# Two elementwise additions of GpSimd, moved from two and three to five and six slots behind their loads

## The chip, the cores and the metric

One core of one Trainium2 chip runs the whole program in one launch. The metric is the time of the execution on the device in microseconds (us), the median over several runs. The kernel before takes 2609.1 us (three runs, 2608.78 to 2609.54).

## What is computed

The reference is a small language-model tower over 64 x 256 = 16384 tokens of width 128, cut here to what matters:

```python
h = take(tok_weight, x)                                # embedding
h = h + linear_attention(layernorm(h))                 # layer 0
h = h + expert_choice_ffn(layernorm(h))                # 32 experts, top 512 tokens each
h = h + causal_attention(layernorm(h))                 # layer 1: 8 heads of width 128, t = 256
# layer 1 feed-forward: each token goes to the 2 best of 8 experts
logits = x @ gate_w + gate_b
w, idx = top_k(logits, 2); w = softmax(w)
out = sum over the two of w * (relu(x @ w1[e] + b1[e]) @ w2[e] + b2[e])
return h + out
```

The last step is the one that the change touches: for each token the two weighted expert rows are added, and the attention's result h is added to that as residual.

## The kernel before

The program is one fixed order per engine, written out by hand, with semaphores between the engines. It has three stages: layer 0 (up to about 900 us), then causal attention and, beside it, layer 1's experts, and a tail in which the last experts run alone.

The second stage is counted in **slots** `u`. Slot u belongs to sequence n = u // 8 and head h = u % 8; two sequences make a group g of 512 tokens (`TG = 4` tiles of 128), so a group is 16 slots. `U = 512` slots hold all heads of all 64 sequences. Every engine has a loop over u and does its part of the slot. For one head: TensorE multiplies the scores (lines 2052, 2053), VectorE takes the maxima (lines 1550, 1551), ScalarE the exponentials (lines 1081, 1083) and refills the mask (line 1091), the rows are scaled by VectorE (lines 1561, 1564; in slots up to 257 GpSimd does this, lines 900 and 901), TensorE transposes them (line 2064), VectorE copies the transposed rows out of the bank (line 1571), and TensorE multiplies them with the values (lines 2076 to 2078). The transposes of one head wait until the copy of the head before is done, so a late line 1571 holds TensorE at line 2064. VectorE also does the norm before attention (small steps in slots with h = 1, 2, 3), and the gate of a finished group (slots with h = 5, 6, 7 of its first and h = 3 to 7 of its second sequence; lines 1213 to 1223 are the steps of an inverse square root, lines 1627 to 1634 the mask, 1640 to 1649 the weights).

The routed rows of a group are scattered by GpSimd to regions of the 8 experts (`scatter`, line 865). The groups are cut into five **portions** (`PORTS`: groups 0 to 13, 14 to 21, 22 to 26, 27 to 29, 30 to 31). When a portion's groups are routed, its **units** (128 rows of one expert) run, one per slot: `place_steps` gives slots 256 to 377 to portion 0, 384 to 457 to portion 1, 464 to 513 to portion 2, and the rest to the tail. For a unit SyncE loads rows and weights four slots ahead (`load_unit`, lines 657 and 659), TensorE multiplies (lines 2092, 2096, 2104), ScalarE and VectorE finish (lines 1117, 1733), and GpSimd scatters the 128 results to `zbuf` two slots behind (`give_unit`, line 880).

When a portion is done, the **results** of its groups are formed. `RESULT_AT` maps a slot to the group c whose data is then loaded: slots 384, 388, ... 436 for groups 0 to 13, and 464, 468, ... 492 for groups 14 to 21 (one every four slots), later ones from slot 526 on. At that slot SyncE runs `turn_result(c)`: it waits until result c-2 is complete, stores it, and issues the loads of group c's expert rows (`zx`, 512 KB, line 687) and of the residual (`h3x`, 256 KB, line 688). GpSimd adds in two steps, each of four instructions of 128 x 128 float32: `add_rows` two slots behind (line 889, waits for the loads), `add_residual` three slots behind (line 895). Both buffers are double (c % 2). Results whose slot is 512 or later are added by VectorE, `LATE = 10` slots behind (lines 1743, 1745).

GpSimd's queue in a slot is, in this order: `residual` at h = 0 (line 874, two instructions that add the output bias for the sequence), `normalise` (early slots only), `scatter` (h = 1 to 4), `give_unit`, `add_rows`, `add_residual`. `give_unit` waits for VectorE's line 1733 of the slot before, so GpSimd follows VectorE slot by slot.

Of the kernel before, what the change touches and what calls it, by code (L numbers as in the profile page):

```python
# [86 lines left out]
def lm_tower(nc, x, L0_tok_weight, L0_attn_Wqkv, L0_attn_temperature, L0_attn_Wproj, L0_attn_bproj,  # L87
# [3 lines left out]
    with ExitStack() as ctx:  # L91
# [391 lines left out]
        def gated(i):  # L483
            return 0 <= i < NG

        STEPS, STEP_AT, STEP_END = place_steps()
        U = NB * H1
# [33 lines left out]
        RESULT_AT = {}  # L521
        for k, (g0, g1) in enumerate(PORTS[:-1]):
            for g in range(g0, g1):
                RESULT_AT[STEP_END[k] + ((6 + 4 * (g - g0)) if k < NKA - 1 else (12 + 6 * (g - g0)))] = g
        LATE = 10
        assert list(RESULT_AT.values()) == list(range(PORTS[-1][0]))

        def rounds(eng, one):
# [196 lines left out]
        def _(pool):  # L725
# [134 lines left out]
            def scatter(g, k, j):  # L860
                if k == 0 and j == 0:
                    pool.wait_ge(twice, 16 * (g + 1))
                    pool.wait_ge(pos_ready, g + 1)
                pool.nop(nofuse=True)
                pool.indirect_dma_start(out=spread_rows, out_offset=bass.IndirectOffsetOnAxis(ap=pos[:, k, j:j + 1], axis=0),  # L865
                                        in_=xr4s[g % 2][:, k, j], in_offset=None).then_inc(spread, 16)

            def residual(n):
                i, p = n // 2, n % 2
                pool.wait_ge(h2_in[p], 16 * (i + 1))  # L870
                if n >= 2:
                    pool.wait_ge(h3_ready, n - 1)
                for j in range(2):
                    ins = pool.tensor_tensor(hb[:, p, j], hx[:, p, j], bo[:], ALU.add)
                ins.then_inc(hb_ready, 1)

            def give_unit(t):
                pool.wait_ge(yu_ready, t + 1)
                pool.nop(nofuse=True)
                pool.indirect_dma_start(out=zbuf, out_offset=bass.IndirectOffsetOnAxis(  # L880
                    ap=xu_at(t)[:, C + 1:XW].bitcast(U32), axis=0), in_=yu[:, t % YR], in_offset=None,
                    bounds_check=2 * NTOK - 1, oob_is_err=False).then_inc(z_out[t % YR], 16)

            def add_rows(c):
                pool.wait_ge(z_in[c % 2], 32 * (c // 2 + 1))
                if c >= 2:
                    pool.wait_ge(out_done[c % 2], 16 * (c // 2))
                for j in range(TG):
                    ins = pool.tensor_tensor(res[:, c % 2, j], zx[:, c % 2, j, 0:C], zx[:, c % 2, j, C:2 * C], ALU.add)
                ins.then_inc(res_step, 1)  # L890

            def add_residual(c):
                pool.wait_ge(res_step, c + 1)
                for j in range(TG):
                    ins = pool.tensor_tensor(res[:, c % 2, j], res[:, c % 2, j], h3x[:, c % 2, j], ALU.add)
                ins.then_inc(res_ready, 1)

            def normalise(u, h):
                pool.wait_ge(rinv_ready, u + 1)
                pool.tensor_scalar(pr[:, u % PRN, 0:P], pr[:, u % PRN, 0:P], rinv[:, h % 4, 0:1], None, ALU.mult)  # L900
                pool.tensor_scalar(pr[:, u % PRN, P:3 * P], pr[:, u % PRN, P:3 * P], rinv[:, h % 4, 1:2], None, ALU.mult)\  # L901
                    .then_inc(pr_ready_pool, 1)

            for u in range(NI * 2 * H1):
                n, h = u // H1, u % H1
                i, p = n // 2, n % 2
                if h == 0 and n < NB:
                    residual(n)
                if 0 <= u - N_LAG < POOL_NORM:
                    normalise(u - N_LAG, (h - N_LAG) % H1)  # L910
                if gated(i - 2) and i <= NG and 1 <= h <= TG:
                    if u - 1 <= U:
                        pool.wait_ge(exp_ready, u - 1)
                    scatter(i - 2, p, h - 1)
                if i == NG + 1 and p == 0:
                    scatter(NG - 1, h // TG, h % TG)
                if u - 2 in STEP_AT and STEPS[STEP_AT[u - 2]][2] is not None:
                    give_unit(STEPS[STEP_AT[u - 2]][2])
                if u - 2 in RESULT_AT and u < U:
                    add_rows(RESULT_AT[u - 2])  # L920
                if u - 3 in RESULT_AT and u <= U:
                    add_residual(RESULT_AT[u - 3])
            for q in range(YR):
                pool.wait_ge(z_out[q], given(UNIT0[NK], q))

# [241 lines left out]
        def _(dve):  # L1167
# [507 lines left out]
            def split(n, p):  # L1675

                dve.wait_ge(xT3_ready, n + 1)
                dve.tensor_tensor(x_part[1][:, p], xT3[:, p], x_part[0][:, p].bitcast(F32), ALU.subtract).then_inc(parts_split, 1)  # L1678
# [58 lines left out]
            def results(c):  # L1737
                p = c % 2
                dve.wait_ge(res_ready, c)
                dve.wait_ge(z_in[p], 32 * (c // 2 + 1))  # L1740
                if c >= 2:
                    dve.wait_ge(out_done[p], 16 * (c // 2))
                dve.tensor_tensor(res[:, p], zx[:, p, :, 0:C], zx[:, p, :, C:2 * C], ALU.add).then_inc(res_step, 1)
                dve.wait_ge(res_step, c + 1)
                dve.tensor_tensor(res[:, p], res[:, p], h3x[:, p], ALU.add).then_inc(res_ready, 1)

            def slots(i):
                for p in range(2):
                    n = 2 * i + p
                    for h in range(H1):  # L1750
# [45 lines left out]
                        for k in range(NK):  # L1796
                            if i == PORTS[k][1] + 1 and p == 0 and h < TABLE_PARTS:
                                table(k, h)
                        if u - LATE in RESULT_AT and u - LATE >= U:
                            results(RESULT_AT[u - LATE])  # L1800
            split(0, 0)
# [413 lines left out]
```

## Time and profile before

| | |
|---|---|
| median of three runs | 2609.1 us (2608.78 to 2609.54) |
| the profiled execution, its own time | 2601.45 us |
| its span, first to last instruction | 2599.7 us |
| TensorE / VectorE / ScalarE / GpSimd busy | 2262.5 / 1832.7 / 1685.6 / 1546.0 us |
| mean granted TensorE clock | 0.941 of full speed |
| line 889, GpSimd | 88 instructions (22 results x 4), 1996.8 to 2389.5 us |
| line 895, GpSimd | 88 instructions, 1999.7 to 2392.4 us |

How to read it: the profile is of one execution. Busy times are sums of instruction durations; an engine that is idle but not awaited costs nothing. The stretch in which GpSimd adds results is 1990 to 2400 us, the tail runs from about 2410 us to the end. TensorE's clock has two levels, 1.2 and 2.4 GHz; a granted clock of 1.00 is the higher one.

### The profile page before, as it was taken

Reading aid. Unit: us, or ns where it says so; the run is one execution under the profiler, and the core shown is the slowest. Engines: PE = TensorE matmul, PEld = TensorE weight load, DVE = VectorE, ACT = ScalarE, POOL = GpSimd, SP = SyncE. Lnnn points to the kernel's source line nnn. Section 1 sums busy time; section 2 is a strip of 40 time slices with the busy share of each in tenths; the row PEclk is TensorE's granted clock in tenths of the full one; section 3 lists DMA queues with packets and bytes.
Section 4 is the critical chain, followed back from the end, with each engine's and each line's share of the span. In section 5 each row is a group of like instructions: output and inputs, shape, how many; then the busy total and the mean of one; then the engine's idle time right before and its main releaser. Section 6 shows DMA issues by size and latency. Waiting matters only on the chain.

```text
span 2599.7 us, 59052 instructions
## 1 busy us (share of the span) xinstructions
PE 2262.5 (87%) x16671; PEld 2024.2 (78%) x16687; DVE 1832.7 (70%) x8212; ACT 1685.6 (65%) x5272; POOL 1546.0 (59%) x1870
## 2 busy tenths in 40 slices
PE   4999877676666599999999999999999999999954
PEld 3887765455555498988989899999999888999854
DVE  4887756644444378888888887877778888888622
ACT  3777654222222377777777778888888777888743
POOL 6444100688888568888888874444444666456553
PEclk9999989777777799999999999999999999999987
DMA  2333200344444521110111126555554776477687
GB/s 81 101 91 98 85 22 1 65 73 74 74 74 74 112 60 35 33 35 30 34 36 31 35 80 164 158 161 153 157 158 139 208 215 199 110 224 218 173 258 241
DMA packets 304259, 283.98 MB, mean 109 GB/s; under 512 B 33931, under 2 KB 252651, under 8 KB 303936
## 3 DMA queue, kind: packets, MB, share of 16 engines
q1 hardware_dynamic: 254144, 211.15, 29.7%
q0 software_dynamic: 46336, 61.16, 10.2%
q10 hardware_dynamic: 3456, 7.89, 1.0%
q8 instruction: 138, 2.26, 0.4%
q14 instruction: 185, 1.52, 0.2%
HBM read 185.85 MB, written 88.43 MB: 106 GB/s over the span
## 4 chain that ended last, share of the span: by engine, by line
PE 53%; POOL 17%; DVE 14%; issue 9%; DMA 4%; SPq 2%; ACT 1%; DVEq 0%; POOLq 0%; ACTq 0%
POOL hbuf L831 8%; PE bank L2053 7%; PE bank L2143 6%; PE bank L2129 6%; PE bank L2064 5%; PE bank L2052 4%; PE bank L2096 4%; PE bank L2104 4%; PE bank L2078 4%; PE bank L2077 4%; PE bank L2076 4%; POOL xe L823 3%; POOL vo_place L791 2%; POOL pc L791 2%; PE bank L1936 1%
## 5 line engine op out<-in xcount | busy, mean ns | idle before, releaser
L880 POOL DMA_INDIRECT zbuf<-pc,kb x248 | 248.7, 1003 | 261.4 <-DVE pc L1733 213.1
L865 POOL DMA_INDIRECT spread_rows<-kb,pos x256 | 254.7, 995 | 167.7 <-DVE pc L1733 82.6
L1081 ACT ACTIVATE pr_place<-bank,nmax 128x128 f32<-128x128 f32 x512 | 188.0, 367 | 186.7 <-DVE nmax L1551 186.2
L2053 PE MATMUL bank<-xT,gT 128*128 128x256 f32 x1024 | 306.8, 381 | 0.0
L1571 DVE COPY pr_place<-bank 128x384 f32<-128x384 f32 x512 | 281.4, 550 | 11.2 <-PE bank L2064 10.6
L2064 PE MATMUL bank<-ident,pr_place 128*128 128x128 f32 x1536 | 252.7, 273 | 29.9 <-DVE pr_place L1571 29.8
L2064 PEld LDWEIGHTS bank<-ident,pr_place 128*128 128x128 f32 x1536 | 195.8, 141 | 100.8 <-POOL pr_place L901 20.0
L1550 DVE TENSOR_REDUCE nmax<-bank 128x1 f32<-128x128 f32 x512 | 143.9, 281 | 181.6 <-PE bank L2053 176.8
L2143 PE MATMUL bank<-wvo_part,x_part 128*128 128x512 f32 x768 | 269.6, 459 | 0.0
L1091 ACT ACTIVATE bank<-causal 128x384 f32<-128x384 f32 x512 | 253.4, 495 | 19.7 <-PE bank L2187 3.6
L2129 PE MATMUL bank<-x_part,wqk_part 128*128 128x256 f32 x1536 | 245.6, 296 | 1.2 <-DVE x_part L1678 1.2
L1083 ACT ACTIVATE pr_place<-bank,nmax 128x256 f32<-128x256 f32 x512 | 242.1, 473 | 0.0
L901 POOL TENSOR_SCALAR pr_place<-pr_place,rinv 128x256 f32<-128x256 f32 x256 | 235.7, 921 | 0.0
L831 POOL DMA_INDIRECT hbuf<-ye,idx x128 | 204.0, 1594 | 45.6 <-issue 38.1
L900 POOL TENSOR_SCALAR pr_place<-pr_place,rinv 128x128 f32<-128x128 f32 x256 | 155.3, 607 | 123.4 <-DVE rinv L1557 118.2
L823 POOL DMA_INDIRECT xe<-xrow,idx x128 | 125.2, 978 | 165.8 <-DVE idx L1470 127.7
L1154 ACT ACTIVATE vo_place<-bank 128x512 f32<-128x512 f32 x256 | 153.2, 598 | 105.4 <-PE bank L2143 103.1
L1551 DVE TENSOR_REDUCE nmax<-bank 128x1 f32<-128x256 f32 x512 | 212.1, 414 | 0.0
L2052 PE MATMUL bank<-xT,gT 128*128 128x128 f32 x1024 | 203.0, 280 | 2.8 <-ACT gT L1151 2.5
L2129 PEld LDWEIGHTS bank<-x_part,wqk_part 128*128 128x128 f32 x1536 | 199.9, 190 | 1.8 <-DVE x_part L1678 1.6
L2076 PE MATMUL bank<-vo_place,pr_place 128*128 128x128 f32 x1024 | 198.5, 276 | 0.0
L2077 PE MATMUL bank<-vo_place,pr_place 128*128 128x128 f32 x1024 | 198.2, 275 | 0.0
(336 smaller groups left out, 6518.8 us busy)
## 6 DMA issues: line engine op xcount, KB each, us to landing
pa<-bundle SPq DMA_DIRECT2D x198, 321.0 KB
wu_more<-bundle SPq DMA_DIRECT2D x66, 321.0 KB
junk<-zbuf SPq DMA_DIRECT2D x32, 512.0 KB
kb<-spread_rows SPq DMA_DIRECT2D x248, 65.0 KB
xrow<-xr SPq DMA_DIRECT2D x32, 320.0 KB, 2.4
hbuf<-h SPq DMA_DIRECT2D x32, 256.0 KB, 3.1
hx<-hbuf SPq DMA_DIRECT2D x64, 128.0 KB
h3buf<-h SPq DMA_DIRECT2D x64, 128.0 KB
```

What stands on the lines that cost most here:

```text
L831: pool.indirect_dma_start(out=hbuf, out_offset=bass.IndirectOffsetOnAxis(ap=idx[:, q, c:c + 1], axis=0), in_=ye[:, p, c], in_offset=None, ...
L865: pool.indirect_dma_start(out=spread_rows, out_offset=bass.IndirectOffsetOnAxis(ap=pos[:, k, j:j + 1], axis=0), in_=xr4s[g % 2][:, k, j], ...
L880: pool.indirect_dma_start(out=zbuf, out_offset=bass.IndirectOffsetOnAxis(ap=xu_at(t)[:, C + 1:XW].bitcast(U32), axis=0), in_=yu[:, t % YR] ...
L1091: act.activation(bank[SBANK[u % 2]][:, 0:3 * P], causal[:], ACT.Copy).then_inc(mask_set, 1)
L1571: dve.tensor_copy(prT[:, h % 2], bank[TBANK][:, 0:3 * P]).then_inc(prT_ready, 1)
L2052: pe.matmul(s2[:, 0:P], g[:, 0:P], xT3[:, p, 0:P], start=False, stop=True, skip_group_check=True)
L2053: pe.matmul(s2[:, P:3 * P], g[:, P:2 * P], xT3[:, p], start=False, stop=True, skip_group_check=True)\
L2064: ins = pe.transpose(bank[TBANK][:, k * P:(k + 1) * P], pr[:, u % PRN, k * P:(k + 1) * P], ident[:])
L2076: pe.matmul(o[:, 0:P], prT[:, h % 2, 0:P], v0, start=(h == 0), stop=False, skip_group_check=True)
L2077: pe.matmul(o[:, P:2 * P], prT[:, h % 2, P:2 * P], v0, start=False, stop=False, skip_group_check=True)
L2129: ins = pe.matmul(bank[GBANK][:, k * 2 * P:(k + 1) * 2 * P], wqk_part[a][:, h + k], x_part[b][:, p], start=(m == 0), stop=(m == 2))
L2143: ins = pe.matmul(bank[VBANK][:, :], x_part[b][:, p, (h % 2) * P:(h % 2 + 1) * P], wvo_part[a][:, 4 * (h // 2):4 * (h // 2) + 4], start=(m ...
```

## The change

A constant `ADD_LATE = 5` is added. `add_rows` for a result runs five slots behind the issue of its loads instead of two, `add_residual` six instead of three. The two conditions that cut off results of slot 512 and later now test the result's own slot; they choose the same 22 results. Nothing else changes: the loads, the stores, the number and size of instructions, and all other engines' programs.

```diff
-        LATE = 10
+        LATE, ADD_LATE = 10, 5
...
-                if u - 2 in RESULT_AT and u < U:
-                    add_rows(RESULT_AT[u - 2])
-                if u - 3 in RESULT_AT and u <= U:
-                    add_residual(RESULT_AT[u - 3])
+                if u - ADD_LATE in RESULT_AT and u - ADD_LATE < U:
+                    add_rows(RESULT_AT[u - ADD_LATE])
+                if u - ADD_LATE - 1 in RESULT_AT and u - ADD_LATE - 1 < U:
+                    add_residual(RESULT_AT[u - ADD_LATE - 1])
```

## Rows read from the trace of the kernel before

**Rows 1.** The page: busy us (share of the span) and instructions of each engine.
```profile
PE 2262.5 (87%) x16671; PEld 2024.2 (78%) x16687; DVE 1832.7 (70%) x8212; ACT 1685.6 (65%) x5272; POOL 1546.0 (59%) x1870
```

**Rows 2.** Windows: us from:to, length, busy us (instructions) per engine, clock, DMA share, GB/s.
```profile
1728.00:1784.00 56.00, 56.00 (x457) 53.34 (x456) 44.00 (x208) 47.28 (x166) 25.66 (x29) 1.00 0.58 157
1992.00:2054.00 62.00, 58.67 (x470) 54.95 (x469) 51.73 (x213) 48.80 (x172) 39.09 (x60) 1.00 0.77 220
...
2115.00:2176.00 61.00, 56.42 (x432) 52.58 (x431) 50.78 (x199) 44.93 (x160) 37.48 (x58) 0.94 0.74 213
2292.00:2350.00 58.00, 56.33 (x458) 53.23 (x457) 49.85 (x208) 47.35 (x166) 40.95 (x64) 1.00 0.80 232
```

**Rows 3.** Waits, 1990 to 2400 us: engine, line, awaited: us, times, longest.
```profile
PE bank L2064 <- DVE pr_place L1571: 14.6, 13, 3.0
...
POOL pc L889 <- DMA pc<-h3buf: 30.7, 14, 5.6
...
SPq L679 <- POOL pc L895: 1.6, 4, 0.6
```

**Rows 4.** Timeline of VectorE: start us, duration us, engine, line, operation, out<-in.
```profile
2101.30 0.35 DVE L1733 SCALAR_TENSOR_TENSOR pc<-pa,kb,pc 128x128 f32<-128x128 f32 x1
...
2103.18 2.50 DVE L1561 TENSOR_SCALAR pr_place<-pr_place,rinv 128x128 f32<-128x128 f32 x1
```

**Rows 5.** Timeline of GpSimd beside it.
```profile
2102.47 0.99 POOL L880 DMA_INDIRECT zbuf<-pc,kb  x1 [1.35 <-DVE pc L1733]
2103.48 1.70 POOL L895 TENSOR_TENSOR pc<-pc 128x128 f32<-128x128 f32 x4
2105.14 0.85 POOL L874 TENSOR_TENSOR hb<-hx,bo 128x128 f32<-128x128 f32 x2
```

**Rows 6.** Timeline of TensorE at line 2064; in brackets the idle time before it.
```profile
2046.19 0.30 PE L2064 MATMUL bank<-ident,pr_place 128*128 128x128 f32 x1 [3.01 <-DVE pr_place L1571]
...
2070.47 0.30 PE L2064 MATMUL bank<-ident,pr_place 128*128 128x128 f32 x1 [1.03 <-DVE pr_place L1571]
...
2106.76 0.41 PE L2064 MATMUL bank<-ident,pr_place 128*128 128x128 f32 x2 [2.47 <-DVE pr_place L1571]
...
2131.85 0.30 PE L2064 MATMUL bank<-ident,pr_place 128*128 128x128 f32 x1 [1.25 <-DVE pr_place L1571]
...
2168.21 0.87 PE L2064 MATMUL bank<-ident,pr_place 128*128 128x128 f32 x3 [2.76 <-DVE pr_place L1571]
...
2335.32 0.41 PE L2064 MATMUL bank<-ident,pr_place 128*128 128x128 f32 x2 [1.67 <-DVE pr_place L1571]
```

**Rows 7.** Windows of 5 us around the third of these gaps, columns as in rows 2.
```profile
2165.00:2170.00 5.00, 2.24 (x11) 1.83 (x11) 5.00 (x12) 4.29 (x16) 2.98 (x7) 0.75 0.31 93
2170.00:2175.00 5.00, 5.00 (x23) 4.53 (x23) 2.27 (x14) 1.86 (x6) 2.39 (x3) 0.57 0.85 238
```

**Rows 8.** Timeline of VectorE in a period without results (units run).
```profile
1841.21 0.34 DVE L1733 SCALAR_TENSOR_TENSOR pc<-pa,kb,pc 128x128 f32<-128x128 f32 x1
...
1845.31 0.35 DVE L1733 SCALAR_TENSOR_TENSOR pc<-pa,kb,pc 128x128 f32<-128x128 f32 x1
...
1870.73 0.35 DVE L1733 SCALAR_TENSOR_TENSOR pc<-pa,kb,pc 128x128 f32<-128x128 f32 x1
...
1871.59 0.28 DVE L1561 TENSOR_SCALAR pr_place<-pr_place,rinv 128x128 f32<-128x128 f32 x1
...
1873.15 0.35 DVE L1733 SCALAR_TENSOR_TENSOR pc<-pa,kb,pc 128x128 f32<-128x128 f32 x1
...
1878.52 0.85 DVE L1561 TENSOR_SCALAR pr_place<-pr_place,rinv 128x128 f32<-128x128 f32 x1
```

**Rows 9.** Timeline of VectorE while line 889 runs (2068.54 to 2070.22).
```profile
2068.51 1.34 DVE L1223 SCALAR_TENSOR_TENSOR r<-r 128x4 f32<-128x4 f32 x1
```

**Rows 10.** Timeline of VectorE while lines 895 and 874 run (2391.11 to 2393.67).
```profile
2391.06 2.31 DVE L1733 SCALAR_TENSOR_TENSOR pc<-pa,kb,pc 128x128 f32<-128x128 f32 x1
```

**Rows 11.** Timeline of SyncE's queue in slot 416, the store of a result.
```profile
2109.22 0.45 SPq L679 DMA_DIRECT2D out_dram<-pc  x1
```

## The prediction

> **What bounds the kernel now.** I read the page's busy times first, then TensorE's in a stretch like the changed one but without results, then who waited for whom where the change acts. TensorE is 87% busy over the span, the next engine 70% [rows 1]. In the stretch 1728 to 1784 us, where the expert units run beside attention and no result is added yet, it is busy for 56.00 of 56.00 us [rows 2]. So from there on time is lost only where TensorE is made to stand, or where its clock is lowered. The next rows of that view lie in the two result stretches: TensorE stands for 3.3 and 4.6 us in two windows of the first, and for 1.7 us in one of the second [rows 2]. The view of waits says for whom: between 1990 and 2400 us it has one entry, line 2064 (transposes of the softmax rows) waiting for VectorE's copy of line 1571, 14.6 us in 13 times [rows 3]. GpSimd waited 30.7 us for the loads at line 889, and SyncE 1.6 us for GpSimd's second addition, line 895 [rows 3].
>
> Slots are counted as in the loops: the 22 results that GpSimd adds have their loads issued at slots 384, 388, ... 436 and 464, 468, ... 492. I write "place n" for a slot's remainder by 16. A place is about 3.5 us long (56 by 16).
>
> **Why GpSimd matters to TensorE.** The step that I looked for is VectorE's multiply of line 1561. It takes 0.28 us where GpSimd reads no buffer [rows 8], but 2.50 us at 2103.18 [rows 4]. GpSimd's row beside it shows what was running: line 895 from 2103.48 for 1.70 us, and line 874 directly after it to 2105.99 [rows 5]; line 1561 ends at 2105.68, and the copy of line 1571 that TensorE wants stands behind it in VectorE's queue. So a VectorE operation from buffer to buffer waits while GpSimd reads and writes buffers. TensorE then resumes at 2106.76 after 2.47 us [rows 6]. Three sisters of this gap are 3.01, 2.76 and 1.67 us; all four, 9.9 us, lie at place 15 to 0, where `add_residual` (slot load+3) meets `residual` (line 874, every eighth slot) without anything between. Next come 1.03 and 1.25 us after place 6, where line 889 holds a small root step of the norm for 1.34 us, just ahead of the copy [rows 6, 9]. That hold turned into a gap nearly whole, so place 6 has next to no slack. The other seven waits share 14.6 - 12.2 = 2.4 us.
> The third of the large gaps ends inside a lowered clock: 0.75 of full speed in the window from 2165 and 0.57 in the next, that is some 6.8 us at the lower level (1.2 GHz) after TensorE had stood since 2165.4 [rows 7]. Its cost is 5 x 0.25 + 5 x 0.43 = 3.4 us. The present cost of the results is thus 14.6 + 3.4 = 18.0 us, and that is the most that any placing could win.
>
> **The change, part by part.** Nothing is added or removed: 22 x 4 instructions of line 889 and as many of line 895, at 0.42 to 0.43 us each in a run of four (1.7 us), move three slots later. Loads, stores and their queue stay at their slots, and the changed conditions select the same 22 results (last load slot 492, so no result falls between 509 and 512).
> *The wait for the loads* (30.7 us of GpSimd) goes, as three slots are over 10 us and GpSimd's waits on a load were 5.6 us at most [rows 3]. It is worth nothing by itself: TensorE's one entry is for VectorE, and SyncE's for GpSimd is 1.6 us [rows 3]. What is late next is GpSimd's own work, `give_unit`, that waits for VectorE.
> *The release of SyncE.* `turn_result(c)` needs the residual of c-2, now done at the load's slot + 6, two slots before SyncE asks. Take slot 416, where SyncE stores at 2109.22 [rows 11]. The residual in question would run at slot 414, so before GpSimd's transfer of slot 415, which the trace has at 2102.47 [rows 5]. Even if that were pushed back by a whole addition, 1.7 us, 5.0 us stay. Cost 0; from such a lag of GpSimd on, the wait would hold the unit loads queued behind it on SyncE, and with them TensorE.
> *Where the runs fall.* Line 889 moves from places 2, 6, 10, 14 to 5, 9, 13, 1, and line 895 from 3, 7, 11, 15 to 6, 10, 14, 2. Line 874 stays at 0 and 8, so the eleven joined runs of 2.5 us become 1.7 and 0.9 us apart. A run begins when GpSimd has issued its unit's transfer, 1.8 us after line 1733 ended VectorE's slot (2101.30 + 0.35 to 2103.48) [rows 4, 5].
> (A) Place 15: only line 874 is left beside line 1561. Alone it held that line for 0.85 us in all [rows 8], so 2.50 - 0.85 = 1.65 us go from each of the four gaps, all of which are larger: 6.6 us won. The bounds are nothing and the whole 9.9.
> (B) Place 13 is new, with line 889 starting 1.8 us into a slot that takes 2.4 in a free period (line 1733 at 1870.73 and again at 1873.15 [rows 8]). The copy for TensorE comes early in a slot, but line 1733 would wait. The nearest row is the same line held for 2.31 us by a joined run [rows 10]; by a run of 1.7 I take 1.4 us. Against it stands that line 895 no longer arrives late in place 12, where it held VectorE about as long before the same gaps. These cancel at four places; at the fifth (slot 495) the old run caught nothing that TensorE needed, so up to 1.1 us is new, of which I take 0.5. Bounds 0 and 5 x 1.96 less the old 4 x 1.4, 4.2 us.
> (C) Place 6 gets line 895 in place of line 889, the same run at the same point. Six slots lie there (390, 406, 422, 438, 470, 486), and the old line made a gap at two, 1.03 and 1.25, together 2.3 us; it came late to others, having waited for a load at 14 of its 22 starts [rows 3]. The new one waits for none; I take four gaps of 1.14 us, 4.6 - 2.3 = 2.3 us lost. Bounds: 0 and 6 x 1.25 - 2.3 = 5.2.
> (D) Of the 2.4 us in small gaps, those behind line 895 at places 4 and 12 go, as it no longer runs there: 0.9 us won, an estimate between 0 and 2.4. Places 1, 2, 9 and 10 lie before VectorE's waits for TensorE, which are most of the 12 us that it is idle in a free period (44.0 busy of 56.0 [rows 2]), and cost nothing; if that cover were gone they would cost up to 1.4 us each.
> (E) With no gap over 1.5 us the lowered clock at 2167 should not come: 3.4 us won, bounds 0 and 3.4. But gaps of 3.01 and 2.47 us passed without one, so this is the least certain term.
> Sum: 6.6 - 0.5 - 2.3 + 0.9 + 3.4 = 8.1 us. The profiled execution took 2601.45 us (span 2599.7), so it would become 2593.4; the timed runs have a median of 2609.1, 7.6 longer, and I take the same 8.1 from it: 2601.0 us.
>
> **What a page says against this.** The Trainium skill, "SBUF — State Buffer", section "Who interferes with whom", says that VectorE in a two-port mode and GpSimd exclude each other for the whole instruction, whoever issues first. By instruction, a held line 1561 would slip in after one GpSimd addition, 0.4 us, and parting the runs would be worth nothing. The row of 2.50 us disagrees [rows 4, 5]: the hold lasted to near the end of six instructions. It is a rival below.
>
> **Rivals.** (1) The hold is by instruction, and the four large gaps come from VectorE's backlog at places 14 and 15, which the new runs at 13 and 14 keep up. For: the gaps exceed the 2.2 us hold. Against: the 2.50 us row. Then A and E vanish; D's gain and part of C's loss nearly cancel: 2609 us. Chance 0.12.
> (2) The gaps shrink as said but the low clock comes anyway, or isn't there in the timed runs: 8.1 - 3.4 = 4.7 us, 2604.4. Chance 0.17.
> (3) Slower: line 889 at place 5, directly before the tightest place. It ends 3.5 us into a slot whose line 1733 starts at 3.7 or 3.8 (1841.56 to 1845.31 [rows 8]). If GpSimd is some 2 us late there, the run holds line 1733 for its whole 1.7 us, and place 6 has no slack to give it back: 6 x 1.7 = 10.2 us, with place 13 held for 1.96 instead of 1.4 another 2.8. So 13.0 - 8.1 = 4.9 slower: 2614.0. Against: GpSimd has nothing but its transfer at places 4 and 5 and isn't held by loads any more. Chance 0.13.
> (4) More than forecast: VectorE, less late, misses the runs at 14 and 6 too; A whole, D whole, E: 15.7 less 0 to 3 us, about 2595. Chance 0.13.
>
> **The numbers.** The forecast has 0.45. About 0.2% (5.2 us) is what a measurement can tell from no change. Faster: forecast and (4), 0.58. Same: (1) and (2), 0.29. Slower 0.13. The range from 2596.0 to 2612.0 takes in the bounds of A to E except the joint extremes: it leaves out the end of (4) and most of (3), under 0.2.
>
> **What would show it.** Right: no wait of GpSimd for the load at line 889; no VectorE row of line 1561 over 1.8 us; the gaps before line 2064 at the turn to place 0 at 0 to 1.4 us, those at place 6 of about 1 us up to six times; PE clock 1.00 from 1990 to 2400; SyncE's wait for line 895 still under 3 us. Wrong: gaps of 2 us and more at other places, or SyncE waiting for GpSimd. The prediction also fails if the tail, where TensorE waits for loads, doesn't move forward with the stretch before it.

## The result, and the profile after

The changed kernel takes 2613.8 us (median of 13 runs, 2610.05 to 2616.07), the kernel before, on the same chip, 2608.8 us (13 runs). The ratio is 1.0024, with a 95% interval of 1.0014 to 1.0035: 0.24% slower, where 0.3% faster was forecast. One run of the kernel before took 4396.64 us, far above its other twelve (2599.89 to 2614.88), and the ratio leaves it out; the means of the rest differ by 6.2 us. The profiled execution of after took 2616.07 us (span 2614.3). It is 14.6 us longer than the profiled one of before, which was 7 us short of its own median, so the pair of profiles overstates the loss. In the stretch of the results (between two copies of line 1571, the one numbered 384 and the one numbered 511, counted from 0) before took 450.1 us and after 460.0, which is 9.9 us; the other 4.7 lie 2.8 ahead of it, where only the additions of the first result went away, and 1.9 behind it, where nothing was changed.

The page and the waits of the stretch, in the columns of [rows 1] and [rows 3]:

```profile
PE 2262.5 (87%) x16671; PEld 2023.1 (77%) x16687; DVE 1854.1 (71%) x8212; ACT 1687.5 (65%) x5272; POOL 1550.8 (59%) x1870
...
PE bank L2064 <- DVE pr_place L1571: 23.0, 15, 2.6
PE bank L2181 <- DVE mask L1634: 1.6, 5, 0.4
...
POOL zbuf L880 <- DVE pc L1733: 102.7, 53, 3.1
```

TensorE does the same work in the same time as in [rows 1]. VectorE has the same 8212 instructions but 21.4 us more busy time, so its instructions were **held** longer. An instruction is called held here when it takes longer beside GpSimd's work than it does elsewhere. TensorE's wait at line 2064 is 23.0 us where it was 14.6 [rows 3], and a new one of 1.6 us stands at line 2181 (the gate's matmul with the mask of line 1634). GpSimd's wait for the loads and SyncE's wait for line 895 are both gone.

The turn to place 0 (the remainder of a slot by 16 is called its place, as before), where [rows 4 to 6] had a hold of 2.50 us and gaps up to 3.01:

```profile
2048.08 0.86 DVE L1561 TENSOR_SCALAR pr_place<-pr_place,rinv 128x128 f32<-128x128 f32 x1
2048.37 0.89 POOL L874 TENSOR_TENSOR hb<-hx,bo 128x128 f32<-128x128 f32 x2
...
2050.03 0.52 PE L2064 MATMUL bank<-ident,pr_place 128*128 128x128 f32 x3 [1.31 <-DVE pr_place L1571]
```

Line 1561 fell to 0.86 us, as forecast. But the gaps are 1.31, 1.31, 1.30, 1.31 and 1.30 us, five of them and all alike. What makes them stands two slots earlier, in place 13:

```profile
2039.57 1.80 DVE L1627 CAST topf<-topi 128x8 f32<-128x8 uint32 x1
2040.04 1.30 POOL L889 TENSOR_TENSOR pc<-junk 128x128 f32<-128x128 f32 x3
```

(The row has three of the four instructions of line 889; the fourth follows from 2041.28.) Line 889 holds line 1627, a step of the gate that takes 0.17 us in the period without results; here it takes 1.80. From the copy for TensorE ahead of it to the next one it is 4.3 us, and 2.9 in a period without results.

And places 5 and 6, where most of the loss is:

```profile
2006.51 0.98 POOL L880 DMA_INDIRECT zbuf<-pc,kb  x1 [2.00 <-DVE pc L1733]
2006.86 2.02 DVE L1561 TENSOR_SCALAR pr_place<-pr_place,rinv 128x128 f32<-128x128 f32 x1
2007.32 1.69 DVE L1564 TENSOR_SCALAR pr_place<-pr_place,rinv 128x256 f32<-128x256 f32 x1
2007.50 1.82 POOL L889 TENSOR_TENSOR pc<-junk 128x128 f32<-128x128 f32 x4
2008.94 0.54 DVE L1571 COPY pr_place<-bank 128x384 f32<-128x384 f32 x1
...
2012.97 1.46 DVE L1223 SCALAR_TENSOR_TENSOR r<-r 128x4 f32<-128x4 f32 x1
2013.11 1.69 POOL L895 TENSOR_TENSOR pc<-pc 128x128 f32<-128x128 f32 x4
2014.35 0.54 DVE L1571 COPY pr_place<-bank 128x384 f32<-128x384 f32 x1
...
2015.04 0.52 PE L2064 MATMUL bank<-ident,pr_place 128*128 128x128 f32 x3 [2.57 <-DVE pr_place L1571]
```

In place 5 line 889 holds lines 1561 and 1564, ahead of the copy of line 1571, which comes 4.4 us after the one before it; in a period without results that is 3.0. TensorE has other work there and makes no gap. But VectorE comes 1.4 us late to place 6, and there line 895 holds line 1223, again ahead of the copy. TensorE then stands for 2.57 us. All six such places do it (2.57, 2.58, 2.58, 2.58, 2.10, 2.57: 15.0 us), where before had two gaps, 1.03 and 1.25 [rows 6].

The clock, windows of 5 us in the columns of [rows 2]:

```profile
2195.00:2200.00 5.00, 2.42 (x12) 2.30 (x12) 4.93 (x16) 3.00 (x13) 3.40 (x6) 0.74 0.34 99
2200.00:2205.00 5.00, 5.00 (x38) 4.77 (x38) 4.49 (x18) 3.54 (x12) 1.92 (x4) 0.92 0.59 169
...
2366.00:2371.00 5.00, 2.79 (x13) 2.82 (x14) 4.93 (x17) 2.87 (x10) 3.38 (x8) 0.71 0.39 106
2371.00:2376.00 5.00, 5.00 (x40) 4.77 (x39) 4.26 (x18) 3.66 (x12) 1.41 (x3) 0.95 0.56 152
```

It falls to the lower level twice, for 3.4 us each, at the end of two of the new gaps. 5 x 0.26 + 5 x 0.08 + 5 x 0.29 + 5 x 0.05 = 3.4 us, as much as the one longer dip of before [rows 7] cost.

### The profile page after: what moved, and what is told of

Same layout as the page of the kernel before. It is cut to its first block, busy times and chain, and to the rows that moved or that the text cites. A ratio compares the mean times of both kernels' runs of the same rounds, so it can differ in the third digit from the quotient of the medians.

```text
span 2614.3 us, 59052 instructions
## 1 busy us (share of the span) xinstructions
PE 2262.5 (87%) x16671; PEld 2023.1 (77%) x16687; DVE 1854.1 (71%) x8212; ACT 1687.5 (65%) x5272; POOL 1550.8 (59%) x1870
## 4 chain that ended last, share of the span: by engine, by line
PE 56%; POOL 15%; DVE 14%; issue 8%; DMA 3%; ACT 1%; SPq 1%; ACTq 0%; DVEq 0%; POOLq 0%
POOL hbuf L831 7%; PE bank L2053 7%; PE bank L2143 7%; PE bank L2129 6%; PE bank L2064 6%; PE bank L2052 4%; PE bank L2096 4%; PE bank L2104 4%; PE bank L2077 4%; PE bank L2078 4%; PE bank L2076 4%; POOL xe L823 3%; POOL vo_place L791 2%; PE bank L1936 1%; DVE pr_place L1571 1%
## 5 line engine op out<-in xcount | busy, mean ns | idle before, releaser
L1091 ACT ACTIVATE bank<-causal 128x384 f32<-128x384 f32 x512 | 253.5, 495 | 19.7 <-PE bank L2187 3.6
```

Of the source, the lines that this page charges most:

```text
L1091: act.activation(bank[SBANK[u % 2]][:, 0:3 * P], causal[:], ACT.Copy).then_inc(mask_set, 1)
```

## The experiments

The theory after the first look: a back-to-back run (one instruction directly behind the other) of GpSimd additions is one hold of VectorE, and its price is set by the slack of the place at which it falls; places 5 with 6, and place 13, have none. Rivals: VectorE slips in between GpSimd's instructions and only the backlog counts; any six-slot lag does it; or not the additions but the transfers beside them.

Runs stood on several chips. On two of them the kernel before takes 4 and 5% longer (2720 and 2743 us), and the others 4 to 6% longer. All ratios are to the kernel before on the same chip, and waits are compared only between chips of like speed.

### One slot later, all of them

```diff
-        LATE, ADD_LATE = 10, 5
+        LATE, ADD_LATE = 10, 6
```

> Both additions one slot later still: line 889 at places 6, 10, 14, 2 and line 895 at 7, 11, 15, 3 (the slot's remainder by 16), the very places of the kernel before, but long after the loads have landed. Theory P (the places decide, because an addition holds VectorE and only some places have slack): the six gaps of 2.58 us before line 2064 that the changed kernel has behind places 5 and 6 shrink to 1.0 to 1.3 us, the runs at place 15 join line 874 again and bring back gaps of 2.5 to 3 us there, five of them; TensorE idle at line 2064 some 20 us against 23.0 in the changed kernel and 14.6 in the one before, time 2609 to 2614 us. Theory L (lateness itself costs, by SyncE waiting for the residual of the result two back): SyncE waits for line 895 for 5 us or more in total, and the time is above the changed kernel's 2613.8 us.

2608.9 us, ratio 1.0010 (0.9999 to 1.0020), so not told apart from the kernel before. TensorE's wait at line 2064 is 19.7 us, and SyncE waits for line 895 once, for 0.5 us, where Theory L had 5 or more. Line 889 now falls in place 6 and line 895 in place 15, directly ahead of line 874:

```profile
2104.64 2.48 DVE L1561 TENSOR_SCALAR pr_place<-pr_place,rinv 128x128 f32<-128x128 f32 x1
2104.93 1.69 POOL L895 TENSOR_TENSOR pc<-pc 128x128 f32<-128x128 f32 x4
2106.59 0.85 POOL L874 TENSOR_TENSOR hb<-hx,bo 128x128 f32<-128x128 f32 x2
...
2108.21 0.87 PE L2064 MATMUL bank<-ident,pr_place 128*128 128x128 f32 x3 [2.57 <-DVE pr_place L1571]
```

The large gaps of before are back (2.15, 2.57, 2.16, 2.15, 2.30), without any wait for a load. The six at place 6 are 0.82 to 1.37, 6.3 us in all: a run at place 6 with none at place 5 costs about what the prediction gave it, 1.14 each.

### The six results whose runs fall in places 5 and 6

In `e2_move56` both runs of the six results loaded at place 0 go to places 3 and 4; in `e3_move5` only line 889 moves, to place 3, and line 895 stays in place 6; in `e6_five_alone` line 889 stays in place 5 and line 895 of these six is cut to one column, so that these six results lack most of their residual.

```diff
+        ROWS_AT = {s + (3 if s % 16 == 0 else 5): c for s, c in RESULT_AT.items() if s < U}
+        REST_AT = {s + (4 if s % 16 == 0 else 6): c for s, c in RESULT_AT.items() if s < U}
...
+                if u in ROWS_AT:
+                    add_rows(ROWS_AT[u])
+                if u in REST_AT:
+                    add_residual(REST_AT[u])
```

> The changed kernel, except that the results whose load slot is a multiple of 16 (six of the 22) are added three and four slots behind, at places 3 and 4, in place of 5 and 6. Theory P: the six gaps of 2.58 us go and at most 0.5 us each comes in their place; the gaps of 1.31 us at place 15 stay; TensorE idle at line 2064 falls from 23.0 to some 9 us, time about 2600 us (13 to 15 below the changed kernel). Theory L, or any in which the sum of the additions counts and not their place: six of 22 results restored to nearly the old distance give back at most a quarter of the 5 us difference, 2612 us or more.

> As the run before this one, but of those six results only line 889 is moved (place 3 in place of 5); line 895 stays at place 6. It parts the two members of the pair. Theory P with the pair adding up: line 895 alone leaves gaps of 1.0 to 1.3 us behind place 6, six times, so TensorE idle at line 2064 is about 16 us and the time some 2606 to 2608 us. If one member alone makes the whole gap: either still 2.6 us (line 895) or nearly none (line 889).

```diff
-                for j in range(TG):
-                    ins = pool.tensor_tensor(res[:, c % 2, j], res[:, c % 2, j], h3x[:, c % 2, j], ALU.add)
+                for j in range(TG if c not in SHORT else 1):
+                    m = C if c not in SHORT else 1
+                    ins = pool.tensor_tensor(res[:, c % 2, j, 0:m], res[:, c % 2, j, 0:m], h3x[:, c % 2, j, 0:m], ALU.add)
```

> The changed kernel, but for the six results whose load slot is a multiple of 16 the second addition (line 895, place 6) is cut to one instruction of one column, so these six results miss most of their residual. Line 889 stays at place 5. The counterpart of the run with line 895 alone at place 6, which left gaps of 1.04 to 1.35 us. If the two members simply add up, 2.58 us is 1.3 for each: gaps of about 1.3 us behind place 5 or 6, six of them, TensorE idle at line 2064 some 15 us, time about 2600 us. If line 889 at place 5 only hurts together with line 895, the gaps are under 0.5 us and the time about 2596 us.

> The same kernel as in the run with line 889 alone at place 5 (for six results the second addition is one column only), on this chip. On the other chip its gap before line 2064 behind place 5 or 6 could not be told from the chip's own gaps. If the members of the pair add up: six gaps of about 1.3 us in place of 2.58, TensorE's waits at line 2064 8 us less than in the unaltered changed kernel. If line 889 at place 5 hurts only in company: gaps under 0.5 us, 13 us less.

> Once more line 889 alone at place 5 (six results' second addition cut to one column). On the slower chip the unaltered changed kernel had gaps of 1.5 to 1.6 us at place 6 where the profiled one had 2.58, and this form had 0.4 to 1.0. On a chip like the first: if the members of the pair add up, six gaps of 1.2 to 1.4 us and a ratio to the kernel before of about 0.998; if line 889 hurts only in company, gaps under 0.5 us and 0.996.

`e2_move56` 2599.2 us, 0.9968 (0.9957 to 0.9978). `e3_move5` 2599.5 us, 0.9975 (0.9964 to 0.9986). `e6c` 2599.8 us, 0.9979 (0.9969 to 0.9989); the same kernel on the two longer-running chips gave 1.0008 (0.9991 to 1.0025) and 1.0002 (0.9986 to 1.0017), the second beside 1.0038 (1.0016 to 1.0059) for the unaltered changed kernel, with intervals that overlap. There the unaltered kernel's six gaps at place 6 were 1.0 to 1.6 us and not the 2.5 that were expected:

> The changed kernel itself, unaltered, on the same chip as the three that follow, because the four runs before went to a chip on which the kernel before takes 2742.7 us. Expected: 1.001 to 1.0035 of the kernel before, and in its profile the six gaps of 2.5 us behind place 6 and the five of 1.3 us at place 15.

The waits of `e3_move5` and one of its gaps at place 6 (its lines are two further on than those of after), then the same of `e6c` (three further on):

```profile
PE bank L2066 <- DVE pr_place L1573: 14.1, 14, 1.3
...
2009.09 1.44 DVE L1225 SCALAR_TENSOR_TENSOR r<-r 128x4 f32<-128x4 f32 x1
2009.22 1.69 POOL L897 TENSOR_TENSOR pc<-pc 128x128 f32<-128x128 f32 x4
...
2011.15 0.52 PE L2066 MATMUL bank<-ident,pr_place 128*128 128x128 f32 x3 [1.35 <-DVE pr_place L1573]
```

```profile
PE bank L2067 <- DVE pr_place L1574: 13.7, 14, 1.3
...
2008.45 0.21 POOL L898 TENSOR_TENSOR pc<-pc 128x1 f32<-128x1 f32 x1
...
2008.82 0.52 PE L2067 MATMUL bank<-ident,pr_place 128*128 128x128 f32 x3 [1.02 <-DVE pr_place L1574]
```

With line 895 alone the six gaps are 0.82 to 1.35 (6.5 us), with line 889 alone 1.01 to 1.14 (6.2 us), with both 15.0. So each of the pair costs about 1 us of TensorE at each of the six places, and together 2.3 us more in all than the sum. Taking either away is worth about 9 us of waits. The clock stayed at the higher level from 1990 to 2420 us in all three.

Two expectations were missed. `e3_move5` is 7 to 9 us faster than expected, and can't be told from `e2_move56`. And in `e2_move56` the gaps at place 6 didn't all fall below 0.5 us: four of 0.98 to 0.99 stand there, and the waits at this line are 11.9 us and not 9. Line 895 comes late out of place 4 and holds line 1561 of place 5: in one case its run lasts from 2064.14 to 2065.85, and line 1561 takes 1.54 us beside it. But 16 of the 22 results keep lags of five and six there, and the kernel is faster than before all the same. So the lag isn't what costs.

### Place 13 as well

All results loaded at places 0 and 8 get lags of three and four, so nothing falls in places 5, 6, 13 or 14; `e10` gives those loaded at place 0 a lag of seven for line 895 (place 7), as the one at place 4 arrives late in place 5.

```diff
+        ROWS_AT = {s + (3 if s % 8 == 0 else 5): c for s, c in RESULT_AT.items() if s < U}
+        REST_AT = {s + (4 if s % 8 == 0 else 6): c for s, c in RESULT_AT.items() if s < U}
```

> Every second result (load slots that are multiples of 8) is added three and four slots behind, the others five and six: all runs lie at places 1 to 4 and 9 to 12, where VectorE has idle time behind it, none at 5, 6, 13, 14, 15. Theory P: TensorE idle at line 2064 between 1990 and 2420 us is under 6 us, no lowered clock there, and the time is about 2595 us, below both kernels. If the sum of the additions counts and not their place: 2609 to 2614 us.

> The kernel with all runs at places 1 to 4 and 9 to 12, again, beside the next one on the same chip. Expected 0.994 of the kernel before.

```diff
+        REST_AT = {s + (7 if s % 16 == 0 else 4 if s % 8 == 0 else 6): c for s, c in RESULT_AT.items() if s < U}
```

> As the run with places 1 to 4 and 9 to 12 only, but for results with a load slot that is a multiple of 16 line 895 goes from place 4 to place 7. In that run line 895 arrived late from place 4 in place 5 and left five gaps of 0.8 us. At place 7 VectorE's lines 1561 and 1564 are over before GpSimd's run starts (joined runs there left no gap above 0.31 us in the kernel before). Theory P: those gaps go, TensorE's waits at line 2064 fall from 7.4 to about 4 us, and the time is some 3 us below that run's 0.9941 of the kernel before, 0.993. Rival: SyncE, which asks for this residual one slot later, waits for it and holds the unit loads; then SyncE's waits for line 895 exceed 3 us and the time is no better.

> The kernel with line 895 at place 7 in place of 4 for every fourth result, again. If it is better than the one before it by the gaps that it takes away (5 x 0.8 us less what it adds), it is 0.001 to 0.0015 below it; if the gaps were hidden by something else, the two are equal.

`e4_3and5` 2592.3 us, 0.9941 (0.9928 to 0.9955), with 7.1 us of waits where under 6 were expected, and again as `e4b` 2591.5 us, 0.9946 (0.9928 to 0.9964). `e10` 0.9944 (0.9924 to 0.9963) on a longer-running chip, and 2587.1 us, 0.9924 (0.9907 to 0.9941) as `e10b`; the intervals of the last two ratios overlap, but on their one chip each of the four runs of `e10b` was faster than each of the four of `e4b`. The waits of `e4b`, then of `e10b`:

```profile
PE bank L2066 <- DVE pr_place L1573: 6.6, 10, 1.2
```

```profile
PE bank L2066 <- DVE pr_place L1573: 3.1, 6, 1.0
```

With nothing in places 13 and 14 the five gaps of 1.3 us at the turn to place 0 are gone, though line 874 still runs there. So they and the 1.6 us at line 2181 came from the additions at places 13 and 14 and from nothing at place 15. The two weren't tried apart; in the trace of after the long hold is that of line 1627 in place 13, while no VectorE instruction beside line 895 at 2044.33 to 2046.03, in place 14, takes over 0.6 us. SyncE never waited for line 895 in the stretch of `e10b`, with a lag of seven.

### Is it one hold, or four?

`e7_one_each` makes each addition one instruction of 128 x 512; `e8` (`e8_apart`, `e8b`, `e8c`) keeps four, and GpSimd waits for its own last one before it issues the next. Lags are five and six, as in the change.

```diff
-                for j in range(TG):
-                    ins = pool.tensor_tensor(res[:, c % 2, j], res[:, c % 2, j], h3x[:, c % 2, j], ALU.add)
-                ins.then_inc(res_ready, 1)
+                pool.tensor_tensor(res[:, c % 2], res[:, c % 2], h3x[:, c % 2], ALU.add).then_inc(res_ready, 1)
```

> The changed kernel with each addition as one instruction of 128x512 in place of four of 128x128, at the same places. The run stays about 1.6 to 1.7 us. Theory R (GpSimd's instructions back to back act as one hold): VectorE is held as long as now (line 1561 at place 5 about 2.0 us), gaps of 2.5 us, time within 2 us of 2613.8. Theory I (the hold is by instruction, and four short ones let VectorE in between): one long instruction holds longer, so the gaps grow and the time rises above 2616 us.

```diff
+            def part(ins):
+                ins.then_inc(apart_step, 1)
+                apart[0] += 1
+                pool.wait_ge(apart_step, apart[0])
...
+                    if j < TG - 1:
+                        part(ins)
```

> The changed kernel with a wait of GpSimd for its own last instruction between the four of each addition, so that they don't stand back to back. Theory R: VectorE gets in between two of them, line 1561 and line 1564 at place 5 are held 0.5 us each at most, the gaps of 2.58 and 1.31 us fall below 1 us, and the time falls to about 2600 us although GpSimd's runs get longer. Theory I, or if the gap between them is too short for VectorE: the holds stay at 1.7 us or become longer with the run, time 2614 us or more.

> The same kernel as in the run with the four instructions of each addition set apart by a wait for the one before, on this chip. On the other chip it took 1.0026 of the kernel before, and the form with one long instruction 1.0095. Theory R (back to back they act as one hold): 5 us or more faster than the unaltered changed kernel here, no VectorE operation of lines 1561 and 1564 above 1.0 us at place 5, gaps below 1.2 us. If setting them apart does nothing: within 2 us of it.

> Once more the four instructions of an addition set apart. On the slower chip: 1.0004 of the kernel before against 1.0038 of the unaltered changed kernel, waits at line 2064 of 10.2 against 19.5 us. On a chip like the first I expect the waits to fall from 23.0 us to 8 to 12 and a ratio of about 0.998.

`e7_one_each` 1.0095 (1.0073 to 1.0118), the slowest of all. `e8_apart` beside it 1.0026 (1.0006 to 1.0046); `e8b` 1.0004 (0.9981 to 1.0027) beside 1.0038 of the unaltered one, where the intervals overlap: on those chips inconclusive. `e8c`, on a chip of the first one's speed, 2589.6 us, 0.9935 (0.9918 to 0.9952). Place 6 of `e7_one_each` (VectorE's and TensorE's lines are four back, so 1217 is 1221; line 892 is 895), then the waits and places 5 and 6 of `e8c` (1573, 1583, 2076 are 1561, 1571, 2064; GpSimd's 897 and 905 are 889 and 895):

```profile
2115.16 1.06 POOL L880 DMA_INDIRECT zbuf<-pc,kb  x1 [3.19 <-DVE pc L1729]
2115.60 1.95 DVE L1217 TENSOR_TENSOR r<-r 128x4 f32<-128x4 f32 x1
2116.23 1.28 POOL L892 TENSOR_TENSOR pc<-pc 128x512 f32<-128x512 f32 x1
...
2118.36 0.52 PE L2060 MATMUL bank<-ident,pr_place 128*128 128x128 f32 x3 [2.77 <-DVE pr_place L1567]
```

```profile
PE bank L2076 <- DVE pr_place L1583: 5.9, 13, 0.7
...
2004.22 0.73 DVE L1573 TENSOR_SCALAR pr_place<-pr_place,rinv 128x128 f32<-128x128 f32 x1
2004.90 2.10 POOL L897 TENSOR_TENSOR pc<-junk 128x128 f32<-128x128 f32 x4
2005.01 0.54 DVE L1583 COPY pr_place<-bank 128x384 f32<-128x384 f32 x1
...
2009.19 2.29 POOL L905 TENSOR_TENSOR pc<-pc 128x128 f32<-128x128 f32 x4
...
2009.83 0.52 PE L2076 MATMUL bank<-ident,pr_place 128*128 128x128 f32 x3 [0.16 <-DVE pr_place L1583]
```

One instruction of 1.28 us held line 1217 for 1.95 us; four back to back held line 1561 for 2.02 (after). Set apart, the four take longer (2.1 to 2.3 us) and yet line 1573 takes 0.73 where its counterpart took 2.02. No VectorE instruction beside these additions takes over 0.46 us more than the median of its line, which is less than one addition (0.48); in after it is up to 1.76 us more. The longest of the stretch, 1.27 us (after 2.04), stands beside the two back-to-back instructions of line 874, which were not set apart, as does the 1.19 of the kernel below that has no additions. The wait falls from 23.0 to 5.9 us at unchanged places, more than was expected (8 to 12). That is the direct evidence that the run, not the sum of GpSimd's work, is what holds.

`e7_one_each` came out the way that Theory I, the rival, had it: its instruction is shorter than the run of four, and its gaps at place 6 are 1.6 to 2.9 us, where the unaltered kernel on the other longer-running chip had 1.0 to 1.6. The traces show a difference between one and four. The single instruction let the held VectorE instruction end 0.03 to 0.29 us after its own end, four back to back let it end 0.31 to 0.44 us before the end of the run, when the fourth had just begun. And VectorE was held for over 1 us beside 39 of the 44 single instructions, but beside 28 of the 44 runs of after. So four instructions are not quite one hold, though far nearer to it than to four. Why the single one catches VectorE more often was not tried.

The Trainium skill, "SBUF — State Buffer", section "Who interferes with whom", has the lock last for one instruction. The set-apart run (at most 0.46 us of hold) agrees with it, and so does `e7_one_each` as to the end of the hold; the back-to-back run does not, as the held instruction got nothing before the fourth.

### Both remedies, and no additions at all

`e11_both` has the places of `e10` and the instructions set apart as `e8`. `e5` is the changed kernel with each addition cut to one instruction of one column, all waits and signals kept; its 22 results are not summed.

```diff
-                for j in range(TG):
-                    ins = pool.tensor_tensor(res[:, c % 2, j], zx[:, c % 2, j, 0:C], zx[:, c % 2, j, C:2 * C], ALU.add)
-                ins.then_inc(res_step, 1)
+                pool.tensor_tensor(res[:, c % 2, 0, 0:1], zx[:, c % 2, 0, 0:1], zx[:, c % 2, 0, C:C + 1], ALU.add)\
+                    .then_inc(res_step, 1)
```

> The changed kernel with both remedies: the additions of the six results with slot%16==0 at places 3 and 7, those with slot%16==8 at places 11 and 12, the rest five and six behind; and between the four instructions of each addition GpSimd waits for its own last one. Theory (a back-to-back run of GpSimd is one hold of VectorE, priced where the place has no slack): the remaining waits at line 2064 between 1990 and 2420 us fall from 3.5 us of the places alone to about 2 us, no gap over 0.7 us, no half-speed stretch of the clock, slots 384 to 511 take about 432 us, ratio 0.991 to 0.992. Rival (setting apart only stretches each run, 1.7 to 2.2 us, and helps just where places are bad): waits stay at 3.5 us or grow, ratio 0.9925 to 0.994.

> The changed kernel with the 22 results' additions cut to one instruction of one column each (lines 889 and 895), so the results are not summed; loads, stores and waits stay. It measures what the additions cost in all. The prediction set the present cost in the kernel before at 18.0 us (14.6 of waits and 3.4 of clock). If all of VectorE's holds come from them, TensorE's waits at line 2064 between 1985 and 2410 us fall to 1 to 3 us and the time to about 2590 us. If loads, stores and their waits cost as well, it stays above 2600 us.

> The changed kernel with every addition of lines 889 and 895 cut to one instruction of one column; the rest of each addition is left out, all waits and signals stay. Theory: this is the whole price of the additions; waits at line 2064 fall from 23.0 to 1 to 2 us, slots 384 to 511 take about 432 us, ratio 0.991 to 0.993. Rival (transfers or GpSimd's other work cost as well in this stretch): waits over 4 us remain and the slots take 438 us or more, ratio 0.995 to 0.997.

`e5_no_add`, on the longest-running chip, 0.9969 (0.9954 to 0.9985). `e5b` 2584.2 us, 0.9903 (0.9886 to 0.9920). `e11_both`, beside it, 2584.3 us, 0.9904 (0.9886 to 0.9921). Waits and the window of the stretch, first of `e5b`, then of `e11_both`, then the window of after:

```profile
PE bank L2062 <- DVE pr_place L1569: 1.1, 3, 0.4
...
1990.00:2420.00 430.00, 428.90 (x3460) 406.35 (x3459) 339.96 (x1606) 360.57 (x1260) 200.04 (x252) 1.00 0.71 203
```

```profile
PE bank L2078 <- DVE pr_place L1585: 1.1, 3, 0.4
...
1990.00:2420.00 430.00, 428.94 (x3458) 406.10 (x3457) 356.32 (x1604) 359.31 (x1260) 273.38 (x384) 1.00 0.71 203
```

```profile
1990.00:2420.00 430.00, 405.48 (x3213) 379.36 (x3213) 376.81 (x1501) 336.68 (x1173) 252.42 (x368) 0.99 0.67 193
```

TensorE is busy for 428.9 of 430 us in both, 405.5 in after. The stretch takes 429.7 us without additions and 430.1 with all of them, well placed and set apart. So the additions can be had for nothing, and `e11_both`, 1% under before, is the kernel to keep. It also clears the transfers: DMA's share is higher in both (0.71) than in after (0.67), and TensorE waits for VectorE's copy for 1.1 us and for nothing else.

## Why the prediction was wrong, step by step

Gaps of before and after in the stretch, by the terms of the prediction (us of TensorE, profiled executions):

| term | forecast | before | after | measured |
|---|---|---|---|---|
| A and B, places 13 to 0 | 6.1 won | 9.9 | 6.5 + 1.6 | 1.8 won |
| C, place 6 | 2.3 lost | 2.3 | 15.0 | 12.7 lost |
| D, small gaps | 0.9 won | 2.4 | 1.5 | 0.9 won |
| E, clock | 3.4 won | 3.4 | 3.4 | 0 |
| sum | 8.1 won | 18.0 | 28.0 | 10.0 lost |

**Right:** the bound (TensorE waits for VectorE's copy, VectorE for GpSimd); the wait for loads gone and worth nothing (GpSimd's entry vanished while TensorE's grew); SyncE's release free, even at a lag of seven; the hold of line 1561 at place 15 down from 2.50 to 0.86, forecast 0.85; D, though its exact match is in part luck: 1.4 us of small gaps went, and one of 0.38 us came at 1990 us, ahead of the first addition.

**C, the step that failed.** It priced line 895 in place 6 and had no term for line 889 in place 5: the sum puts it at nothing, and gives no reason. Measured, the pair costs 15.0 us where the sum had 4.6: 6.5 by line 895 alone (`e3_move5`), 6.2 by line 889 alone (`e6c`), and 2.3 by their meeting. The lone run at place 6 was well priced: 1.14 each forecast, 0.82 to 1.37 in `e1_late6` and `e3_move5`, though it came at all six places, not four. Line 889 in place 5 stood only in rival (3), and there with the wrong instruction (line 1733) and under a condition, 2 us of lateness of GpSimd, that wasn't needed. The one sentence on where the copy stands is in step B, for place 13: that it comes early in a slot, ahead of a run that starts 1.8 us into it. Nothing checks it for place 5, and there it doesn't hold. The trace of before had it, in the slot that starts at 1841.56:

```profile
1842.36 0.97 POOL L880 DMA_INDIRECT zbuf<-pc,kb  x1 [1.98 <-DVE pc L1733]
1842.72 0.28 DVE L1561 TENSOR_SCALAR pr_place<-pr_place,rinv 128x128 f32<-128x128 f32 x1
1842.91 0.54 DVE L1564 TENSOR_SCALAR pr_place<-pr_place,rinv 128x256 f32<-128x256 f32 x1
1843.37 0.54 DVE L1571 COPY pr_place<-bank 128x384 f32<-128x384 f32 x1
```

GpSimd's transfer ends at 1843.33, and there a run would begin; line 1564 ends at 1843.45, 0.1 us too late to be safe, and the copy comes behind it. And the hold begins earlier than the run (below), so that line 1561, which ends at 1843.00, is not safe either. In after both lines are caught, for 2.02 and 1.69 us.

**B, mis-sized.** It took 1.4 us of hold at place 13 against as much that line 895 used to cost in place 12, and called it even at four places. Measured: line 1627 held for 1.80, five gaps of 1.3 us and five small ones at line 2181, 8.1 us in all. The even count would have left four gaps at 1.36, 0.82, 1.11 and 0.02 (those of [rows 6] less 1.65); three came out larger. The fifth, priced at 0.5, came whole, 1.30. `e4` and `e10` show where they come from: with places 13 and 14 empty, all ten are gone. Forecast and outcome agree on A's hold; the gain that it should have brought was taken back by the hold in place 13, whose price B took as paid already.

**E.** No gap over 1.5 us was the condition, and C broke it. In the kernels that met it (`e2`, `e3`, `e4`, `e6c`, `e8c`, `e10b`) the clock didn't fall in the stretch. There the term was right, and it depended on C. It isn't a rule for all chips: on the longest-running one the clock fell in `e5_no_add` and twice in `e8_apart` behind single gaps of 0.99 and 1.02 us, between 1990 and 2420 us.

**The rivals.** Rival (1), a hold of one instruction, falls by the rows of after, where line 1561 is held across three of four, and by `e8c`. Rival (2) had the gaps shrink as forecast, which they didn't, so it was not tried. Rival (4) falls by the outcome. Rival (3) named the place and the sign, and its total, 2614.0, is near the 2613.8 measured, but by offsetting errors: it had 13.0 of loss against 8.1 of gain, where the trace has 12.7 in C alone against 2.7 of gain. It had 0.13; read with the rows above it should have led. The statement that 18.0 us is the most that any placing could win counted TensorE's waits and the clock only. With no additions the stretch is 20.4 us shorter than before (450.1 to 429.7), and with both remedies 20.0, so the bound was some 2 us too low. Placing alone (`e10b`) won 16.9 us of the stretch; its median is 18.6 us below that of before, with an interval on both sides of 18.0.

**What stays open.** The profiles differ by 9.9 us in the stretch, the timed medians by 5.0, and the ratio makes it 6.2 (3.7 to 9.1 by its interval). The profiled execution of before was 7 us under its median; in which part a median run of it loses those, no trace here shows. Why the pair costs 2.3 us more than its two members was not tried either. It isn't the low clock, as the gaps are alike with a dip (2.58, 2.57) and without (2.57, 2.58, 2.58, 2.10). An estimate that fits: line 889 makes VectorE 1.4 us late and alone leaves a gap of 1.0, so 0.4 us of slack takes up the rest; the pair has this slack only once, and 6 x 0.4 = 2.4 us.

## What to carry to other kernels

Before moving work on an engine that can hold another one, list for each slot where its run will start and which instruction of the other engine stands there, for every place and not for the one to be cleared: two neighbouring places that each cost 1 us cost 2.6 together. Price a run of short GpSimd instructions as one hold about as long as the run, which begins and ends some 0.4 us earlier than it, and let GpSimd wait for itself between them where VectorE feeds the bottleneck. An early experiment that cuts the suspected work to one column gives the bound of all placings, and tells when to stop.

## What the runs showed of the hardware that was not expected

- A back-to-back run of GpSimd instructions holds a VectorE instruction from buffer to buffer across nearly all of it: 2.02 us by four of 0.47 to 0.57, 2.32 to 2.50 by six (before), 1.95 by one of 1.28. With a self-wait between the four, line 1561 took 0.28 to 0.74 us at place 5, and nothing beside the additions was held for over 0.5.
- The hold begins before the addition's record. In `e7_one_each` line 1217 started at 2115.60, 0.63 us before the addition and while GpSimd's transfer was being issued; it takes 0.16 us elsewhere, but it didn't end before 2117.55. In after, line 1561 started 0.64 us before the addition and takes 0.28 elsewhere. So both were held some 0.4 us before the addition's record starts. A transfer with no addition behind it didn't hold line 1561 at 1842.72 (0.28 us). What in the transfer or the addition does it, no run here shows.
- In the stretch, on chips of the first one's speed, TensorE's clock fell to the lower level (1.2 GHz), for 3.4 or 6.8 us, only where TensorE had just stood for over 2 us, and not each time: at one of three such gaps of before, at two of six of after, at three of five of `e1_late6`. On the longest-running chip it also fell behind gaps of 0.99 and 1.02 us.
- What a placing costs differed between chips: on one where the kernel before takes 4% longer, the gaps of the changed kernel at place 6 were 1.0 to 1.6 us in place of 2.6. The kernel without additions stood at 0.9969 (0.9954 to 0.9985) on the longest-running chip and at 0.9903 (0.9886 to 0.9920) on a faster one.
